# Expert queues of a routed feed-forward layer: full units of 512 slots, and half units of 256 at each queue's end

## The chip, the cores and the metric

One Trainium2 chip, one core. The metric is the device time of one execution in microseconds (us), the median over the runs shown; lower is better.

## The reference

50,000 rows of 256 numbers go through two layers. First a graph layer adds, to each row, the weighted normalised rows of its edges (25,000 edges, in fp16). Then a mixture of 8 experts is added. What the change touches is the second:

```python
logits = x @ gate_w + gate_b
probs = softmax(logits); idx = argmax(probs); prb = probs[idx]
pos = position of the token among those of its expert
kept = pos < C            # C = ceil(1.25 * 50000 / 8) = 7813
buf[e, pos] = x           # one queue per expert
hmid = relu(buf @ w1[e] + b1[e])      # 256 -> 1024
ybuf = hmid @ w2[e] + b2[e]           # 1024 -> 256
y = nan_to_num(ybuf[idx, pos] * prb * kept)
x = x + y
```

With the inputs of the reference, the eight queues hold 4993, 4159, 7813, 4367, 7813, 7813, 3828 and 2769 tokens (three are cut at C).

## The kernel before

The program has three stages. `edge_and_constants` does the graph layer. `route_tokens` computes logits for 1,024 rows a step and scatters each row, with its mean, its deviation, its token number and its logits, to a slot of its expert's queue in DRAM (`slots`). `run_experts` works the queues off. Only the third stage, and the last few VectorE (DVE) instructions of the second that count the units, are touched by the change.

A **unit** is 512 slots (`UNIT`, four blocks of 128, `SUB`). At the end of `route_tokens` DVE computes for each expert the number of units, ceil(queued / 512), their running sum (`first_unit`), the row at which each queue starts (`first_row`) and the row behind the last token (`first_blank`). For the queues above that is 10, 9, 16, 9, 16, 16, 8 and 6 units, 90 in all.

`run_experts` has one program for each engine, and each walks over experts and units alike: `experts` loads the expert's first and last unit number into registers (L881, L882), then `Fori(begin, end)` runs the body for each unit. The code of an expert stands six times in a row: for expert 0, twice inside a loop that runs two times, and for the last three. The engines meet through semaphores that count units, so nothing but the unit number tells an engine where it is. For unit u:

- **SyncE (SP)** keeps a ring of four units loaded (`load`, L906), and writes 512 blank slots behind the queue of the next expert (`blank_behind`, L900), so that a unit's unused slots have a token number out of range.
- **VectorE (DVE)** first normalises unit u+1 into `hn` (L1024, L1029). It then subtracts, for each of the eight column blocks f of the hidden layer, the rounded half of the hidden values from the full ones (`hlo`, L1047); then `xlo` of unit u+1 (L1036). Once TensorE has finished the second product it does the **tail**: bias (`y`, L1058), times probability (L1063), the three masks and `yo` for nan_to_num (L1067 to L1077), plus the residual (L1079), which releases the scatter.
- **TensorE (PE)** does the first product into `u_H` (L1114): 8 blocks of 6 matmuls with 512 columns, two PSUM buffers deep. Then it transposes unit u+1 (`u_T`, L1099, 8 matmuls), which waits for `hn` of u+1. Then the second product into `u_Y` (L1125): 8 blocks f, each 4 blocks of slots times 3 matmuls with 256 columns, which wait for `hlo`. Each fp32 product is three passes over rounded and rest parts.
- **ScalarE (ACT)** applies relu to each block of `u_H` (`hm`, L999), rounds it (`hhi`, L1003), and rounds the transposed unit u+1 (`xhi`, L983).
- **GpSimd (POOL)** scatters the unit's rows to the output with four indirect transfers (L967) and waits for their landing, which lets DVE overwrite the token numbers. Before the units of expert e it splits the weights of expert e+1: a cast of 128x4096 (`whi`, L943) and a subtraction (`wlo`, L945), then issues the loads of the weights of e+2.

Of the kernel before, what the change touches and what calls it, by code (L numbers as in the profile page):

```python
# [21 lines left out]
ALU = mybir.AluOpType  # L22
ACT = mybir.ActivationFunctionType
# [358 lines left out]
def route_tokens(nc, ctx, t):  # L382
# [66 lines left out]
    offset = sb("offset", [1, E], F32)  # L449
    first_unit, first_row, first_blank = t["first_unit"], t["first_row"], t["first_blank"]  # L450

# [23 lines left out]
    with nc.Block() as block:  # L475
# [149 lines left out]
        def _(v):  # L625
# [144 lines left out]
            v.tensor_reduce(count[:], over[:], AX.X, ALU.add).then_inc(step, n.inc())  # L770
            v.memset(begin[:], 0.0).then_inc(step, n.inc())
            v.wait_ge(step, n.now())
            for e in range(E):
                v.scalar_tensor_tensor(out=begin[:, e + 1:e + 2], in0=count[:, e:e + 1], scalar=1.0,
                                       in1=begin[:, e:e + 1], op0=ALU.max, op1=ALU.add).then_inc(step, n.inc())
                v.wait_ge(step, n.now())
            v.tensor_scalar(offset[:], expert[0:1, :], float(QUEUE), None, ALU.mult).then_inc(step, n.inc())
# [3 lines left out]
            v.wait_ge(step, n.now())  # L781
            v.tensor_copy(first_unit[:], begin[:])
            v.tensor_copy(first_row[:], offset[:])
# [3 lines left out]
def run_experts(nc, ctx, t):  # L787
# [9 lines left out]
    first_unit, first_row, first_blank = t["first_unit"], t["first_row"], t["first_blank"]  # L797
    E, D, F = w1.shape
# [6 lines left out]
    assert KF * D == WF and E >= 6 and E % 2 == 0  # L805
    HUGE = 1e4
# [14 lines left out]
    blank = sb("blank", [P, SUB, W], F32)  # L821
# [55 lines left out]
    def experts(eng, body):  # L877

        def one(e, buf):  # L880
            begin = eng.value_load(first_unit[0:1, bass.ds(e, 1)], min_val=0, max_val=(E - 1) * UMAX)  # L881
            end = eng.value_load(first_unit[0:1, bass.ds(e + 1, 1)], min_val=1, max_val=E * UMAX)  # L882
            body(e, buf, begin, end)
# [4 lines left out]
        for e in range(E - 3, E):  # L888
            one(e, e % 2)

    with nc.Block() as block:

        @block.sync
        def _(sp):
            sp.dma_start(b1r[:], b1.rearrange("e (k p) -> (e k) p", p=P)).then_inc(b1_loaded, 16)

            def blank_behind(e):

                row = sp.value_load(first_blank[0:1, bass.ds(e, 1)], min_val=0, max_val=E * QUEUE - UNIT)
                sp.dma_start(slots[bass.ds(row, UNIT), :].rearrange("(s p) w -> p s w", p=P), blank[:])\  # L900
                    .then_inc(blanked, 16)
# [7 lines left out]
            def expert(e, buf, begin, end):  # L909
# [6 lines left out]
                with sp.Fori(begin, end) as u:  # L916

                    sp.wait_ge(y_ready, u + (1 - RING + SEED["y_ready"]))
                    sp.nop(nofuse=True)
                    load(u, (u * UNIT + at).with_bounds(min_val=0, max_val=E * QUEUE - UNIT))  # L920
# [262 lines left out]
```

## Time and profile before

| | |
|---|---|
| median of 3 runs | 3663.58 us (3653.1 to 3665.04) |
| span of the profiled execution | 3533.8 us |
| PE busy | 2919.1 us (83%) |
| DVE busy | 2291.9 us (65%) |
| ACT busy | 1564.2 us (44%) |
| POOL busy | 1796.0 us (51%) |
| third stage, first to last instruction | about 1338 to 3534 us of the span |

No time of its own is listed for the profiled execution; the span runs from the first to the last instruction on the core, and the median of the runs lies 129.8 us above it. Busy time of a matmul counts from its start to a modelled end, and neighbours overlap; where a pace is wanted it is read from starts.

### The profile page before, as it was taken

The numbers are of one execution on the slowest core, as the hardware profiler recorded it, in microseconds if no ns is written. First come the engines' busy times: TensorE is split into PE (matmuls) and PEld (weight loads), VectorE is DVE, ScalarE is ACT, GpSimd is POOL, SyncE is SP. The second block draws the span as 40 slices with busy tenths as digits, with TensorE's granted clock in tenths as the row PEclk, the third lists the DMA queues.
The fourth block names the chain that finished last, engine by engine and source line by source line (L and its number), as shares of the span: only waits on it lengthen the run. The fifth ranks groups of instructions, "written<-read, shape, count | busy, mean of one in ns | idle before, by whom it ended". The sixth has DMA issues, their size and how long they took to land.

```text
span 3533.8 us, 60004 instructions
## 1 busy us (share of the span) xinstructions
PE 2919.1 (83%) x18982; PEld 2664.8 (75%) x18983; DVE 2291.9 (65%) x5804; ACT 1564.2 (44%) x2603; POOL 1796.0 (51%) x1195
## 2 busy tenths in 40 slices
PE   4544434078888876999999999999999999999998
PEld 3433434078888875988989988888988989998987
DVE  6655455077777764676676676676676676667666
ACT  2322222045555543554454555454555444454453
POOL 4788887647777773334343333434333433334332
PEclk8766666555555557999999999999999999999999
DMA  9544444399999963111111111111111121111110
GB/s 344 135 86 76 90 76 87 29 290 302 306 307 292 281 201 111 49 52 62 55 54 50 49 45 51 62 53 59 49 44 50 42 68 41 49 55 32 49 46 26
DMA packets 303467, 371.32 MB, mean 105 GB/s; under 512 B 35431, under 2 KB 263812, under 8 KB 300080
## 3 DMA queue, kind: packets, MB, share of 16 engines
q1 hardware_dynamic: 221504, 199.21, 19.2%
q0 software_dynamic: 78304, 145.23, 15.4%
q10 hardware_dynamic: 3600, 26.22, 1.8%
q8 instruction: 22, 0.36, 0.0%
q14 instruction: 37, 0.30, 0.0%
HBM read 184.33 MB, written 195.85 MB: 108 GB/s over the span
## 4 chain that ended last, share of the span: by engine, by line
PE 55%; DVE 3%; issue 2%; DVEq 1%; DMA 0%; SPq 0%; POOL 0%; ACT 0%; POOLq 0%; ACTq 0%
PE u_Y L1125 29%; PE u_H L1114 24%; PE u_T L1099 2%; DVE y L1058 1%; DVE yo L1077 1%; DVE yo L1074 0%; DVE y L1063 0%; DVE hn L1029 0%; DVE low L1068 0%; DVE hlo L1047 0%; DVE yo L1072 0%; DMA u_pay<-slots 0%; DMA slots<-blank 0%; DVEq L882 0%; DVEq L881 0%
## 5 line engine op out<-in xcount | busy, mean ns | idle before, releaser
L967 POOL DMA_INDIRECT out_x<-yo,u_token x360 | 712.3, 1979 | 1330.5 <-DVE yo L1079 1243.7
L1125 PE MATMUL u_Y<-whi,hhi 128*128 128x256 f32 x2880 | 816.0, 283 | 2.2 <-DVE hlo L1047 2.2
L999 ACT ACTIVATE hm<-u_H,b1e 128x512 f32<-128x512 f32 x720 | 496.3, 689 | 712.3 <-PE u_H L1114 684.0
L1125 PE MATMUL u_Y<-wlo,hhi 128*128 128x256 f32 x2880 | 807.2, 280 | 0.0
L1125 PE MATMUL u_Y<-whi,hlo 128*128 128x256 f32 x2880 | 806.2, 280 | 0.0
L1114 PE MATMUL u_H<-xhi,whi 128*128 128x512 f32 x1440 | 570.8, 396 | 3.1 <-DVE xlo L1036 2.5
L1114 PE MATMUL u_H<-xlo,whi 128*128 128x512 f32 x1440 | 570.3, 396 | 0.0
L1114 PE MATMUL u_H<-xhi,wlo 128*128 128x512 f32 x1440 | 570.0, 396 | 0.0
L1125 PEld LDWEIGHTS u_Y<-whi,hhi 128*128 128x128 f32 x2880 | 545.1, 189 | 2.4 <-DVE hlo L1047 2.4
L1125 PEld LDWEIGHTS u_Y<-wlo,hhi 128*128 128x128 f32 x2880 | 545.0, 189 | 0.0
L1125 PEld LDWEIGHTS u_Y<-whi,hlo 128*128 128x128 f32 x2880 | 544.3, 189 | 0.0
L534 POOL DMA_INDIRECT slots<-pay,slot_i x392 | 457.5, 1167 | 163.7 <-issue 122.5
L1058 DVE TENSOR_TENSOR y<-u_Y,b2e 128x256 f32<-128x256 f32 x360 | 127.7, 418 | 614.1 <-PE u_Y L1125 614.1
L1003 ACT ACTIVATE hhi<-hm 128x512 fp32r<-128x512 f32 x720 | 456.0, 633 | 22.9
L1047 DVE TENSOR_TENSOR hlo<-hm,hhi 128x512 fp32r<-128x512 f32 x720 | 452.7, 702 | 2.9 <-ACT hhi L1003 2.9
L212 POOL DMA_INDIRECT agg<-sums,target x200 | 328.5, 1642 | 79.2 <-issue 58.8
L599 PEld LDWEIGHTS ps_L<-gw,hT 128*128 128x128 f32 x1568 | 350.3, 332 | 0.1
L614 PE MATMUL ps_T<-ident,h 128*128 128x128 f32 x784 | 208.7, 431 | 167.3 <-ACT h L565 167.3
L599 PE MATMUL ps_L<-gw,hT 128*128 128x8 f32 x1568 | 342.4, 352 | 0.0
L1114 PEld LDWEIGHTS u_H<-xhi,whi 128*128 128x128 f32 x1440 | 271.0, 188 | 65.9 <-issue 4.1
L1114 PEld LDWEIGHTS u_H<-xhi,wlo 128*128 128x128 f32 x1440 | 270.9, 188 | 65.5
L1114 PEld LDWEIGHTS u_H<-xlo,whi 128*128 128x128 f32 x1440 | 271.0, 188 | 61.5
(127 smaller groups left out, 3757.4 us busy)
## 6 DMA issues: line engine op xcount, KB each, us to landing
xt<-in_x SPq DMA_DIRECT2D x49, 1024.0 KB
out_x<-pay SPq DMA_DIRECT2D x49, 1024.0 KB, 6.0
u_pay<-slots SPq DMA_DIRECT2D x91, 534.0 KB, 3.9
agg<-zeros ACTq DMA_DIRECT2D x25, 1024.0 KB, 10.9
at<-agg SPq DMA_DIRECT2D x49, 512.0 KB
raw<-in_L_ffn_w POOLq DMA_DIRECT2D x14, 1024.0 KB, 6.9
src_row<-in_src SPq DMA_DIRECT2D x25, 512.0 KB
slots<-pay,slot_i POOLq DMA_INDIRECT x392
```

The source lines that it names most:

```text
L212: pool.indirect_dma_start(out=agg[:, :], out_offset=bass.IndirectOffsetOnAxis(ap=target[:, r, c:c + 1], axis=0), in_=sums[:, r, c, :], in_ ...
L534: pool.indirect_dma_start(out=slots[:, :], out_offset=bass.IndirectOffsetOnAxis(ap=slot_i[:, r, g:g + 1], axis=0), in_=pay[:, r, g, :], in ...
L599: last = pe.matmul(logits[:, g, :], hT[:, g * KD + kd, :], gw[:, kd, :], start=(kd == 0), stop=(kd == KD - 1))
L614: last = pe.transpose(ps_T[:, n, :], h[:, q, g, kd * P:(kd + 1) * P], ident[:])
L967: pool.indirect_dma_start(out=out[:, :], out_offset=bass.IndirectOffsetOnAxis(ap=token[:, s:s + 1], axis=0), in_=yo[:, s, :], in_offset=No ...
L999: act.activation(hm[:, f, :], ps_H[:, f % 2, :], ACT.Relu, bias=b1e[:, f:f + 1])\
L1003: act.activation(hhi[:, f, :], hm[:, f, :], ACT.Copy).then_inc(hhi_ready, 1)
L1047: v.tensor_tensor(hlo[:, f, :], hm[:, f, :], hhi[:, f, :].bitcast(F32), ALU.subtract)\
L1058: last = v.tensor_tensor(y[:, s, :], ps_Y[:, s, 0:D], b2e[:], ALU.add)
L1099: last = pe.transpose(ps_T[:, k, s * P:(s + 1) * P], hn[:, s, k * P:(k + 1) * P], ident[:])
L1114: last = pe.matmul(ps_H[:, f % 2, :], w1_at(w, buf, k, f), a[:, k, :], start=(j == 0), stop=(j == len(passes) - 1))
L1125: last = pe.matmul(ps_Y[:, s, 0:D], a[:, f, cols], w2_at(w, buf, f), start=(f == 0 and j == 0), stop=(f == KF - 1 and j == 2))
```

## The change

Each queue is now worked off in full units of 512 slots followed by one or two half units of 256. DVE computes, beside the number c of 512-slot units, `wholes` = max(c - 1, 1) and `halves`, which is 2 where the last 512-slot unit would hold more than 256 tokens and else 1. Two new register tables go with it: `half_unit` (the number of the first half unit of each expert) and `half_row` (the row offset for half units). For the queues above the wholes are 9, 8, 15, 8, 15, 15, 7 and 5 (82), and the halves 2, 1, 1, 2, 1, 1, 1 and 1 (10).

Every engine's unit loop becomes two, with the body written out once for each size:

```diff
+    def units(eng, e, begin, end, unit):
+        half = eng.value_load(half_unit[0:1, bass.ds(e, 1)], min_val=1, max_val=E * (UMAX + 1))
+        with eng.Fori(begin, half) as u:
+            unit(u, SUB)
+        with eng.Fori(half, end) as u:
+            unit(u, SUB // 2)
```

In a half unit, first product, relu, rounding and `hlo` use 256 columns instead of 512; the second product, the tail and the scatter do two blocks of slots instead of four. What prepares unit u+1 stays at 512 slots in every unit: the load from `slots`, the normalisation, the eight transposes, `xhi` and `xlo`. The number of eight blocks f, and with it of ACT's and DVE's instructions on them, stays too. The blank stretch behind a queue grows from 512 to 768 slots.

```diff
-    blank = sb("blank", [P, SUB, W], F32)
+    blank = sb("blank", [P, BLANK // P, W], F32)
...
-                row = sp.value_load(first_blank[0:1, bass.ds(e, 1)], min_val=0, max_val=E * QUEUE - UNIT)
-                sp.dma_start(slots[bass.ds(row, UNIT), :].rearrange("(s p) w -> p s w", p=P), blank[:])\
+                row = sp.value_load(first_blank[0:1, bass.ds(e, 1)], min_val=0, max_val=E * QUEUE - BLANK)
+                sp.dma_start(slots[bass.ds(row, BLANK), :].rearrange("(s p) w -> p s w", p=P), blank[:])\
...
+                half = sp.value_load(half_unit[0:1, bass.ds(e, 1)], min_val=1, max_val=E * (UMAX + 1))
+                half_at = sp.value_load(half_row[0:1, bass.ds(e, 1)], min_val=0, max_val=E * QUEUE - UNIT)
+                with sp.Fori(begin, half) as u:
+                    unit(u, u * UNIT + at)
+                with sp.Fori(half, end) as u:
+                    unit(u, u * (UNIT // 2) + half_at)
...
-                    for s in range(SUB):
+                    for s in range(subs):
                         pool.indirect_dma_start(
                             out=out[:, :], out_offset=bass.IndirectOffsetOnAxis(ap=token[:, s:s + 1], axis=0),
                             in_=yo[:, s, :], in_offset=None, bounds_check=N - 1, oob_is_err=False,
-                        ).then_inc(y_sent, 16)
+                        ).then_inc(y_sent, 16 * SUB // subs)
...
-                        act.activation(hm[:, f, :], ps_H[:, f % 2, :], ACT.Relu, bias=b1e[:, f:f + 1])\
+                        act.activation(hm[:, f, cols], ps_H[:, f % 2, cols], ACT.Relu, bias=b1e[:, f:f + 1])\
...
-                        v.tensor_tensor(hlo[:, f, :], hm[:, f, :], hhi[:, f, :].bitcast(F32), ALU.subtract)\
+                        v.tensor_tensor(hlo[:, f, cols], hm[:, f, cols], hhi[:, f, cols].bitcast(F32), ALU.subtract)\
...
-                            last = pe.matmul(ps_H[:, f % 2, :], w1_at(w, buf, k, f), a[:, k, :],
+                            last = pe.matmul(ps_H[:, f % 2, cols], w1_at(w, buf, k, f), a[:, k, cols],
```

At the end of `route_tokens` DVE has ten more instructions on rows of 8 or 128 numbers of one partition.

Where the two loops meet, two places of the instruction streams. **GpSimd, from the scatter of one expert to the split of the next expert's weights** (`TENSOR_LOAD` reads a register from a table, `out_x<-yo` is the scatter). Before:

```order
L967 DMA out_x<-yo,u_token 50000x256 x4
L971 ISA
L963 REGISTER_ALU
L963 COMPARE_AND_BRANCH
L881 TENSOR_LOAD first_unit
L881 ISA x2
L882 ISA
L882 TENSOR_LOAD first_unit
L882 ISA x2
L941 REGISTER_ALU
L943 CAST whi<-raw 128x4096
L944 REGISTER_ALU
```

After, from the last scatter of the full units' loop on:

```order
L921 COMPARE_AND_BRANCH
L923 UNCONDITIONAL_BRANCH
L923 ISA
L1010 DMA out_x<-yo,u_token 50000x256 x2
L1014 ISA
L923 REGISTER_ALU
L923 COMPARE_AND_BRANCH
L907 TENSOR_LOAD first_unit
L907 ISA x2
L908 ISA
L908 TENSOR_LOAD first_unit
L908 ISA x2
```

The last scatter ahead of the cast has two transfers where it had four; the third register load (L920) stands behind the split, so it is not in its way.

**VectorE, the tail of a unit** (from the bias on `y` to the add that releases the scatter), before and then in the half units' loop:

```order
L1058 TENSOR_TENSOR y<-u_Y,b2e 128x256 x4
L1063 TENSOR_SCALAR y<-y,prob 128x256 x4
L1065 REGISTER_ALU
L1067 TENSOR_SCALAR finite<-y 128x1024
L1068 TENSOR_SCALAR low<-y 128x1024
L1071 ISA
L1071 COPY u_token<-u_pay 128x4
L1072 TENSOR_SCALAR yo<-y 128x1024
L1073 REGISTER_ALU
L1074 TENSOR_TENSOR yo<-yo,low 128x1024
```

```order
L1110 TENSOR_TENSOR y<-u_Y,b2e 128x256 x2
L1115 TENSOR_SCALAR y<-y,prob 128x256 x2
L1117 REGISTER_ALU
L1119 TENSOR_SCALAR finite<-y 128x512
L1120 TENSOR_SCALAR low<-y 128x512
L1123 ISA
L1123 COPY u_token<-u_pay 128x4
L1124 TENSOR_SCALAR yo<-y 128x512
L1125 REGISTER_ALU
L1126 TENSOR_TENSOR yo<-yo,low 128x512
```

All of the tail is half as wide, the copy of the token numbers apart; the order is the same.

## Rows read from the trace of the kernel before

**Rows 1.** The page, part 4: chain that ended last, by engine.
```profile
PE 55%; DVE 3%; issue 2%; DVEq 1%; DMA 0%; SPq 0%; POOL 0%; ACT 0%; POOLq 0%; ACTq 0%
```
**Rows 2.** Timeline of DVE, one unit: start us, us, engine line op out<-in xcount [idle before].
```profile
1572.78 1.42 DVE L1058 TENSOR_TENSOR y<-u_Y,b2e 128x256 f32<-128x256 f32 x4 [6.79 <-PE u_Y L1125]
1574.31 1.14 DVE L1063 TENSOR_SCALAR y<-y,prob 128x256 f32<-128x256 f32 x4
1575.48 0.69 DVE L1067 TENSOR_SCALAR finite<-y 128x1024 uint8<-128x1024 f32 x1
...
1578.82 1.37 DVE L1077 COPY_PREDICATED yo<-finite,y 128x1024 f32<-128x1024 uint8 x1
1580.31 1.23 DVE L1079 TENSOR_TENSOR yo<-yo,u_pay 128x1024 f32<-128x1024 f32 x1
1581.76 1.39 DVE L1029 TENSOR_SCALAR hn<-u_pay,scales 128x256 f32 x4
1583.05 4.91 DVE L1047 TENSOR_TENSOR hlo<-hm,hhi 128x512 fp32r<-128x512 f32 x8
...
1596.05 1.42 DVE L1058 TENSOR_TENSOR y<-u_Y,b2e 128x256 f32<-128x256 f32 x4 [6.78 <-PE u_Y L1125]
```
**Rows 3.** Timeline of PE's weight loads (PEld), the same unit.
```profile
1572.47 0.19 PEld L1114 LDWEIGHTS u_H<-xhi,whi 128*128 128x128 f32 x1
...
1583.55 1.02 PEld L1099 LDWEIGHTS u_T<-ident,hn 128*128 128x128 f32 x8
1584.54 0.19 PEld L1125 LDWEIGHTS u_Y<-whi,hhi 128*128 128x128 f32 x1
```
**Rows 4.** Groups of ACT in the third stage, window 1500 to 3534: busy, mean ns.
```profile
L999 ACT ACTIVATE hm<-u_H,b1e 128x512 f32<-128x512 f32 x672 | 463.2, 689 | 678.2 <-PE u_H L1114 651.7
L1003 ACT ACTIVATE hhi<-hm 128x512 fp32r<-128x512 f32 x672 | 425.6, 633 | 21.4
```
**Rows 5.** Timeline of POOL, from expert 1 to expert 2.
```profile
1824.93 5.16 POOL L967 DMA_INDIRECT out_x<-yo,u_token  x1 [0.30 <-issue]
1830.39 0.98 POOL L967 DMA_INDIRECT out_x<-yo,u_token  x1 [0.31 <-issue]
1834.07 3.61 POOL L943 CAST whi<-raw 128x4096 fp32r<-128x4096 f32 x1 [2.70 <-issue]
1837.77 9.13 POOL L945 TENSOR_TENSOR wlo<-raw,whi 128x4096 fp32r<-128x4096 f32 x1
```
**Rows 6.** Timeline of DVE at the same place.
```profile
1838.45 9.39 DVE L1063 TENSOR_SCALAR y<-y,prob 128x256 f32<-128x256 f32 x4
...
1870.59 1.42 DVE L1058 TENSOR_TENSOR y<-u_Y,b2e 128x256 f32<-128x256 f32 x4 [8.66 <-PE u_Y L1125]
```
**Rows 7.** Group of DVE's multiplications, window 1500 to 3534.
```profile
L1063 DVE TENSOR_SCALAR y<-y,prob 128x256 f32<-128x256 f32 x340 | 139.6, 474 | 9.1
```
**Rows 8.** Busy time by stretch: PE, PEld, DVE, ACT, POOL, granted clock, DMA.
```profile
1852.00:1856.00 4.00, 0.15 (x1) 0.15 (x2) 3.73 (x8) 0.00 (x0) 0.92 (x1) 0.50 1.01 340
```
**Rows 9.** Timeline of POOL and of DVE in the first unit of expert 0.
```profile
1367.88 9.33 POOL L945 TENSOR_TENSOR wlo<-raw,whi 128x4096 fp32r<-128x4096 f32 x1
1364.98 15.79 DVE L1047 TENSOR_TENSOR hlo<-hm,hhi 128x512 fp32r<-128x512 f32 x7 [1.27 <-ACT hhi L1003]
```
**Rows 10.** Timeline of POOL, one scatter from expert 0 to expert 1.
```profile
1609.91 1.50 POOL L967 DMA_INDIRECT out_x<-yo,u_token  x1 [0.30 <-issue]
```
**Rows 11.** Chain in order of time, start of the third stage.
```profile
1340.55 4.65 DMA slots<-blank
...
1346.39 0.28 SPq L915
```
**Rows 12.** Timeline of DVE and POOL, last unit.
```profile
3517.30 1.42 DVE L1058 TENSOR_TENSOR y<-u_Y,b2e 128x256 f32<-128x256 f32 x4 [6.78 <-PE u_Y L1125]
3526.83 0.98 POOL L967 DMA_INDIRECT out_x<-yo,u_token  x1 [14.19 <-DVE yo L1079]
...
3530.68 0.98 POOL L967 DMA_INDIRECT out_x<-yo,u_token  x1 [0.30 <-issue]
```

More of the change, by code:

```diff
@@ L781, in _ @@
             v.wait_ge(step, n.now())
+            v.scalar_tensor_tensor(out=half_at[:], in0=wholes[:], scalar=float(t["UNIT"] // 2), in1=offset[:],
+                                   op0=ALU.mult, op1=ALU.add).then_inc(step, n.inc())
+            v.wait_ge(step, n.now())
             v.tensor_copy(first_unit[:], begin[:])
+            v.tensor_copy(half_unit[:], wholes[:])
+            v.tensor_copy(half_row[:], half_at[:])
             v.tensor_copy(first_row[:], offset[:])
@@ L973, in expert @@
                     pool.sem_inc(y_clear, 1)
+                units(pool, e, begin, end, unit)
             experts(pool, expert)
@@ L988, in expert, with unit @@
                 act.nop(nofuse=True)
-                with act.Fori(begin, end) as u:
+                def unit(u, subs):
+                    cols = slice(0, subs * P)
                     act.wait_ge(hn_ready, u + 1)
@@ L1041, in expert, with unit @@
                 v.nop(nofuse=True)
-                with v.Fori(begin, end) as u:
+                def unit(u, subs):
+                    cols = slice(0, subs * P)
                     c = Count(u * PER)
@@ L1056, in expert @@
                     v.wait_ge(second_done, u + 1)
-                    for s in range(SUB):
+                    used = slice(0, subs)
+                    for s in range(subs):
                         last = v.tensor_tensor(y[:, s, :], ps_Y[:, s, 0:D], b2e[:], ALU.add)
@@ L1106, in expert, with unit @@
                 pe.nop(nofuse=True)
-                with pe.Fori(begin, end) as u:
+                def unit(u, subs):
+                    cols = slice(0, subs * P)
                     pe.wait_ge(x_ready, u + 1)
@@ L1121, in expert @@
                         pe.wait_ge(hid_ready, KF * u + (f + 1 + SEED["hid_ready"]))
-                        for s in range(SUB):
-                            cols = slice(s * P, (s + 1) * P)
+                        for s in range(subs):
+                            rows = slice(s * P, (s + 1) * P)
                             for j, (a, w) in enumerate(((hhi, whi), (hhi, wlo), (hlo, whi))):
-                                last = pe.matmul(ps_Y[:, s, 0:D], a[:, f, cols], w2_at(w, buf, f),
+                                last = pe.matmul(ps_Y[:, s, 0:D], a[:, f, rows], w2_at(w, buf, f),
                                                  start=(f == 0 and j == 0), stop=(f == KF - 1 and j == 2))
                     last.then_inc(second_done, 1)
+                units(pe, e, begin, end, unit)
             experts(pe, expert)
```

60 lines of the change are left out of this document (42 added, 18 removed).

## The prediction

> **What bounds the kernel now.** I read the page's chain first: 55% of the span is on PE, 3% on DVE [rows 1]. The change is in the third stage alone, so next comes the timeline of DVE over one unit [rows 2], where two units' first tail instructions lie 1596.05 - 1572.78 = 23.27 us apart. Almost all units have that period. PE's weight loads of the same unit fill it: 11.08 us of first product, 0.99 of transposes, then the second product until the next unit [rows 3]. But one DVE path is just as long. Counted from the start of a tail, the tail and the normalisation end at 1581.76 + 1.39 - 1572.78 = 10.4 us, and the transposes start at 10.8 [rows 2, 3]. So whatever makes DVE late in a full unit makes PE late by as much.
>
> That happens once for each expert. GpSimd splits the next expert's weights: cast and subtraction, until 1846.90 [rows 5]. DVE's multiplication of the tail starts at 1838.45 and takes 9.39 us instead of 1.14, until 1847.84 [rows 2, 6]. It waited for the subtraction, and the unit lasts from its tail at 1836.9 (1.5 before the multiplication, as in rows 2) to the one at 1870.59: 33.7 us, 10.4 too long, 8.25 of them the stall. PE, idle meanwhile, then has a granted clock of 0.50, the 1.2 GHz level [rows 8], so a little is lost on top. Over the stage, 340 such multiplications take 139.6 us [rows 7]; at 1.14 / 4 each they would take 96.9. So **42.7 us of stall** lie in the six splits after expert 0's, and with some 1.5 us of clock loss each (2.1 in the one above) the six units lose about 52.
>
> **The change, part by part.** T is the start of the tail of the unit before, on DVE.
>
> *A half unit behind a full one.* The tail in front is a full one, so the transposes can't start before T + 10.8, as now. The first product of 256 columns is done long before. PE would need 5.5 us; ACT's pair of relu and rounding takes 0.69 + 0.63 = 1.32 us at 512 columns [rows 4], 0.66 if all of it halves, 1.32 if nothing does. Even 8 x 1.32 = 10.6 fits in. So: 10.8 + 0.99 transposes + half of 11.2 for the second product (1584.54 to 1596.05, less 0.3 until DVE has started) + 0.3 = 17.7. PE is idle for some 3.5 us before its transposes. Between no loss and the 1.5 above I add 0.4: **18.1 us** instead of 23.27, bounds 17.7 and 19.2. It is not the 11.6 that half the work suggests.
>
> *A half unit behind a half one.* The tail halves. To the first mask it is 2.70 us, in which eight pieces of 128x256 become four: 1.4. From there to the copy (1575.48 to 1578.82) three masks and an add are halved: 3.34 - 3 x 0.27 - 0.53 = 2.0. The copy and the last add give 0.96 and 0.70 [rows 2]. A = T + 5.1 is when the scatter is released, instead of T + 8.8. Normalisation ends at T + 6.7, transposes can start at T + 7.1. ACT at 0.98 us a block, the middle of its bounds, lets PE finish at T + 7.0. Sum 7.1 + 0.99 + 5.6 + 0.3 = **14.0**.
>
> *Counts.* Six experts swap their last full unit for one half: 6 x (18.1 - 23.27) = **-31**. Experts 0 and 3 swap it for two: 2 x (18.1 + 14.0 - 23.27) = **+17.7**.
>
> *The split moves against DVE.* This is the largest term. Now the last scatter has four transfers, of which one waits 5.16 us for DVE's `hlo` series; the cast starts 2.7 us after the last one ends [rows 5]. In the change, the first transfer starts 0.8 us after A (the last unit: tail at 3517.30, transfer at 3526.83 [rows 12]), that is at T + 5.9; with 1.28 from transfer to transfer the second ends at T + 8.2. DVE is then still in its register loads, a third one now (0.55 us on SyncE [rows 11]), and the normalisation, so `hlo` starts only at about T + 8.9. The cast comes to the lock at T + 11.1. DVE is in the series of eight `hlo`, 4.9 us back to back [rows 2], until T + 13.8. I take it that the cast waits for its end, as the transfer of 5.16 us did. Then the cast runs to T + 17.5 and the subtraction to T + 26.7. The next tail starts at T + 23.8 and multiplies at T + 25.3: a stall of 1.4 us in place of 7.1 in the mean. Six times: 8.4 instead of 52, **-44**. Bounds: 0 if the cast slips in without harm (-52), 7 us each if it blocks `hlo` (below).
>
> *First unit of an expert.* It costs about 1 us over 23.27 now, as DVE has two register loads in the way. Its tail in front is now half as long, so DVE is early; but PE's own third load (0.55) comes between two products. -0.5 each, seven times: **-3.5**.
>
> *Start of the stage.* The blank transfer of 534 KB lands in 4.65 us and the first load waits for it [rows 11]; 801 KB take between 4.65 and 7.0, I take +1.3. Wiping the blank tile: +0.4. Two register loads of SyncE at 0.55: +1.1. Together **+2.8**. DVE's ten new instructions at the end of the second stage lie under GpSimd's last scatters, which keep the stage open some 19 us longer: 0.
>
> *End.* The tail is 3.7 shorter and two transfers of 1.28 fall away: **-6.2** [rows 12].
>
> Sum: -31 + 17.7 - 44 - 3.5 + 2.8 - 6.2 = **-64.2**. Against the profiled execution that is 3533.8 - 64.2 = 3469.6 of span; against the median, 129.8 above the span, 3599.4, say **3600 us**. That the part outside the span stays is an assumption; the program is longer by half on PE.
>
> **Rivals.**
> 1. *The cast breaks into the `hlo` series.* In the first unit of expert 0, seven `hlo` take 15.79 us under cast and subtraction [rows 9]: that is 11.5 more than their 0.61 each, longer than the subtraction's 9.33, so the cast blocks them as well. And one scatter transfer got through a series in 1.50 us [rows 10]. If so, `hlo` of the last three blocks waits until the subtraction ends at T + 24, where PE wants the sixth at T + 19: about 5.6 us idle, plus clock, 7 each in place of 1.4. +33.6: 3633 us. For it: DVE's series is eight instructions, with an edge between each two. Against it: most scatter transfers wait the whole series out, as in rows 5. The Trainium skill ("SBUF — State Buffer", section "Who interferes with whom") says that whoever of the two issues first holds the shared pair for a whole instruction; read strictly, the waiting cast would get in after the `hlo` that is running, which is this rival. The 5.16 us transfer speaks against reading it so.
> 2. *A half unit costs as much as a full one*, since its fixed parts (full preparation of the next unit, ACT's per-instruction part) bound it. Then 8 x 5.2 + 2 x 9.3 = 60 us come back: 3660, no change. ACT's pair would have to take 2.5 us at half the width, against 1.32 now.
> 3. *Slower: the granted clock falls in the half unit and stays down.* In it PE works in bursts (ACT sets the pace) and is then idle until T + 10.8. If the lower level lasted through the half unit's transposes and second product, these 6.6 us would double, and the next first product's 11.1 too: 17.7 us for each of eight experts, 142 in all, 3741 us. It decides the sign from 64 / 8 = 8 us of doubled work for each expert on. Against it: after a longer idle time the level of 0.50 shows [rows 8], and the 10 us lost there are mostly the 8.25 of stall. The Trainium skill ("TensorE: Matmul & The Clock Gate", section "A second HAM failure mode: psum-queue depth-cycling") reports that short pauses between matmul groups on cycling PSUM buffers can make the clock swing. The trace before has no group of this kind; by that section the half units' first product would bring it.
> 4. *The change doesn't do what it says:* no. 82 + 10 units follow from the queues, and the streams show both loops.
>
> **Numbers.** Forecast 0.60 (its own range 3585 to 3617, from the bounds of the half units, 17.7 to 19.2, the split without harm, the start and the runs' spread of some 6 us). Rival 1 0.28. Rival 2 0.04. Rival 3 0.03. Something unlisted, such as code of twelve loops fetched late or a longer part outside the span, 0.05. The range reaches down to 3580 and up to rival 1 with the dearer half unit, 3645. A change of under 0.3% (11 us) can't be told from none here. Faster: forecast, rival 1 and most of the unlisted, 0.92. Same: rival 2 and a little, 0.05. Slower: rival 3, 0.03.
>
> **What the profile of the changed kernel would show.** Tails 23.27 us apart in full units, about 18.1 into the first half unit, 14.0 into the second. Half-width relu and rounding together near 0.98 us. POOL's cast starts some 11 to 14 us after a half tail. DVE's multiplications with full width near 0.3 us in the mean instead of 0.41, none above 2.5 us. If instead `hlo` instructions of over 9 us appear once for each expert, rival 1 holds. A granted clock below 1.00 in more than a short stretch for each half unit speaks for rival 3. Wrong altogether would be tails after half units over 23 us apart, or an unchanged sum of rows 7.

## The result, and the profile after

| | before | changed |
|---|---|---|
| median | 3660.99 us (4 runs) | 3562.68 us (4 runs, 3555.91 to 3572.21) |
| ratio, 95% interval | | 0.9741 (0.9716 to 0.9766) |
| span of the profiled execution | 3533.8 us | 3567.3 us |
| first instruction of the third stage's DVE, in the span | 1338.44 | 1466.00 |
| third stage, from there to the end | 2195.4 us | 2101.3 us |

The change makes the kernel 98 us faster (2.6%). I had forecast 3600 us, 64 us faster, with a range of 3580 to 3645; the measured time lies 17 us below it.

The two profiled executions can't be compared by their spans. The second stage, which the change hardly touches, ends 128 us later in the profile of the changed kernel. Where both kernels were profiled side by side, their third stages start alike (1332.4 and 1332.6 us in the first group of runs below). In two other groups both start later: at 1422 to 1430 us with the kernel before as a basis, at 1417 to 1432 with the changed one. So this difference goes with the group of runs and not with the change; what makes it is not known (the chip's number alone does not: of the two groups on the chip numbered 12, one starts at 1331 to 1335, the other at 1424 to 1432). It also shows that my 129.8 us "around the span" were not around it: each later execution lists a time 1 to 2 us above its span (here 3569.06 to 3567.3). The third stages can be compared (with the tiles of the kernel before at the old distance it took 2194.5 to 2196.0 us in three groups of runs), and they differ by 94 us.

One full unit on DVE, then the first and the second half unit of expert 0, in the timeline of the changed kernel (start us, us, engine line op out<-in xcount, idle time before):

```profile
1653.15 1.42 DVE L1110 TENSOR_TENSOR y<-u_Y,b2e 128x256 f32<-128x256 f32 x4 [6.26 <-PE u_Y L1181]
...
1698.67 1.42 DVE L1110 TENSOR_TENSOR y<-u_Y,b2e 128x256 f32<-128x256 f32 x4 [6.26 <-PE u_Y L1181]
...
1707.58 1.38 DVE L1078 TENSOR_SCALAR hn<-u_pay,scales 128x256 f32 x4
1708.87 2.77 DVE L1098 TENSOR_TENSOR hlo<-hm,hhi 128x256 fp32r<-128x256 f32 x8
...
1717.21 0.76 DVE L1110 TENSOR_TENSOR y<-u_Y,b2e 128x256 f32<-128x256 f32 x2 [4.26 <-PE u_Y L1181]
...
1721.62 0.69 DVE L1131 TENSOR_TENSOR yo<-yo,u_pay 128x512 f32<-128x512 f32 x1
...
1722.54 1.39 DVE L1078 TENSOR_SCALAR hn<-u_pay,scales 128x256 f32 x4
...
1730.77 0.76 DVE L1110 TENSOR_TENSOR y<-u_Y,b2e 128x256 f32<-128x256 f32 x2 [2.85 <-PE u_Y L1181]
```

Against [rows 2]: the first half unit lasts 1717.21 - 1698.67 = 18.5 us, the second 13.6. The normalisation behind a full tail still ends at +10.3, behind a half tail at +6.7. The half tail releases the scatter at 1721.62 + 0.69, +5.1. The first half unit is within the forecast's bounds, the ends of the normalisation are as forecast. But the next tail behind the one at 1653.15 stands at 1675.91: **full units are 22.76 us apart, not 23.27**. PE's weight loads show where the half microsecond went:

```profile
1652.84 0.19 PEld L1170 LDWEIGHTS u_H<-xhi,whi 128*128 128x128 f32 x1
1663.71 0.14 PEld L1153 LDWEIGHTS u_T<-ident,hn 128*128 128x128 f32 x1
...
1664.70 0.19 PEld L1181 LDWEIGHTS u_Y<-whi,hhi 128*128 128x128 f32 x1
...
1675.60 0.19 PEld L1170 LDWEIGHTS u_H<-xhi,whi 128*128 128x128 f32 x1
```

The first product takes 10.87 us for 11.08 [rows 3], the second 10.90 for 11.2, the transposes the same 0.99. No instruction of a full unit differs between the kernels. I had not considered that PE's pace could differ all the same.

The split of the next expert's weights, at the same place as [rows 5, 6], from expert 0's last half unit (tail at 1730.77) on, first GpSimd and then DVE:

```profile
1738.01 0.99 POOL L1010 DMA_INDIRECT out_x<-yo,u_token  x1 [0.30 <-issue]
1742.26 5.62 POOL L985 CAST whi<-raw 128x4096 fp32r<-128x4096 f32 x1 [3.26 <-issue]
1747.96 9.38 POOL L987 TENSOR_TENSOR wlo<-raw,whi 128x4096 fp32r<-128x4096 f32 x1
...
1740.10 8.32 DVE L1098 TENSOR_TENSOR hlo<-hm,hhi 128x512 fp32r<-128x512 f32 x8
...
1754.69 1.42 DVE L1110 TENSOR_TENSOR y<-u_Y,b2e 128x256 f32<-128x256 f32 x4 [4.96 <-PE u_Y L1181]
1756.22 2.07 DVE L1115 TENSOR_SCALAR y<-y,prob 128x256 f32<-128x256 f32 x4
```

The cast comes at +11.5 (forecast +11.1) and lasts 5.62 instead of 3.61: it waits 2.0 us for `hlo`, where the forecast had 2.7. But it gets in ahead of the eighth one: the series takes 8.32 us instead of 4.90. The multiplication is held for under 1 us. Over the stage the group of [rows 7] now reads

```profile
L1115 DVE TENSOR_SCALAR y<-y,prob 128x256 f32<-128x256 f32 x348 | 105.1, 365 | 9.9
```

which is 6 us above 348 times 0.285, where it was 42.7.

In the half units behind full ones PE waits 4.3 us for `hn` and the granted clock goes down at about the end of the wait, to the 1.2 GHz level for part of this stretch (the stretch's mean is 0.71):

```profile
1709.01 0.97 PEld L1153 LDWEIGHTS u_T<-ident,hn 128*128 128x128 f32 x8 [4.31 <-DVE hn L1078]
1708.00:1712.00 4.00, 2.98 (x17) 2.99 (x18) 4.00 (x13) 1.03 (x1) 3.49 (x2) 0.71 0.60 170
```

### The profile page after: what moved, and what is told of

Same layout as the page of the kernel before. It is cut to its first block, busy times and chain, and to the rows that moved or that the text cites. A ratio compares the mean times of both kernels' runs of the same rounds, so it can differ in the third digit from the quotient of the medians.

```text
span 3567.3 us, 60077 instructions
## 1 busy us (share of the span) xinstructions
PE 2846.6 (80%) x18806; PEld 2603.9 (73%) x18807; DVE 2245.0 (63%) x5836; ACT 1539.7 (43%) x2638; POOL 1724.4 (48%) x1183
## 4 chain that ended last, share of the span: by engine, by line
PE 53%; DVE 4%; issue 1%; DVEq 0%; DMA 0%; SPq 0%; ACT 0%; POOL 0%; POOLq 0%; ACTq 0%
PE u_Y L1181 27%; PE u_H L1170 23%; PE u_T L1153 3%; DVE y L1110 1%; DVE yo L1129 1%; DVE yo L1126 1%; DVE y L1115 0%; DVE hn L1078 0%; DVE low L1120 0%; DVE hlo L1098 0%; DVE yo L1124 0%; DMA slots<-blank 0%; DMA u_pay<-slots 0%; DVE scales L1073 0%; DVEq L1078 0%
## 5 line engine op out<-in xcount | busy, mean ns | idle before, releaser
L1010 POOL DMA_INDIRECT out_x<-yo,u_token x348 | 668.5, 1921 | 1261.4 <-DVE yo L1131 1179.5
L1181 PE MATMUL u_Y<-whi,hhi 128*128 128x256 f32 x2784 | 784.2, 282 | 1.5 <-DVE hlo L1098 1.5
L1181 PE MATMUL u_Y<-wlo,hhi 128*128 128x256 f32 x2784 | 775.4, 279 | 0.0
L1046 ACT ACTIVATE hm<-u_H,b1e 128x512 f32<-128x512 f32 (+1 forms) x736 | 487.9, 663 | 639.8 <-PE u_H L1170 627.0
L539 POOL DMA_INDIRECT slots<-pay,slot_i x392 | 415.3, 1059 | 325.5 <-DVE slot_i L748 210.3
L1170 PE MATMUL u_H<-xhi,whi 128*128 128x512 f32 (+1 forms) x1472 | 563.6, 383 | 8.0 <-issue 5.5
L1170 PE MATMUL u_H<-xhi,wlo 128*128 128x512 f32 (+1 forms) x1472 | 562.2, 382 | 0.0
L1170 PE MATMUL u_H<-xlo,whi 128*128 128x512 f32 (+1 forms) x1472 | 560.2, 381 | 0.0
L1050 ACT ACTIVATE hhi<-hm 128x512 fp32r<-128x512 f32 (+1 forms) x736 | 448.7, 610 | 23.3
L1098 DVE TENSOR_TENSOR hlo<-hm,hhi 128x512 fp32r<-128x512 f32 (+1 forms) x736 | 454.0, 692 | 2.9 <-ACT hhi L1050 2.9
L604 PE MATMUL ps_L<-gw,hT 128*128 128x8 f32 x1568 | 344.0, 353 | 39.8 <-ACT hT L566 24.5
L1170 PEld LDWEIGHTS u_H<-xhi,wlo 128*128 128x128 f32 x1472 | 277.4, 188 | 50.4
```

The lines of the kernel that those rows point to most:

```text
L539: pool.indirect_dma_start(out=slots[:, :], out_offset=bass.IndirectOffsetOnAxis(ap=slot_i[:, r, g:g + 1], axis=0), in_=pay[:, r, g, :], in ...
L604: last = pe.matmul(logits[:, g, :], hT[:, g * KD + kd, :], gw[:, kd, :], start=(kd == 0), stop=(kd == KD - 1))
L1010: pool.indirect_dma_start(out=out[:, :], out_offset=bass.IndirectOffsetOnAxis(ap=token[:, s:s + 1], axis=0), in_=yo[:, s, :], in_offset=No ...
L1046: act.activation(hm[:, f, cols], ps_H[:, f % 2, cols], ACT.Relu, bias=b1e[:, f:f + 1])\
L1050: act.activation(hhi[:, f, cols], hm[:, f, cols], ACT.Copy).then_inc(hhi_ready, 1)
L1098: v.tensor_tensor(hlo[:, f, cols], hm[:, f, cols], hhi[:, f, cols].bitcast(F32), ALU.subtract)\
```

## The experiments

Kernels of one group ran on one chip, beside the kernel before. "Stage" is the third stage from its first DVE instruction to the end of the span; "units" the time from the first tail to the last.

### The pace of PE: four kernels on one chip

**The kernel before, again** (no edit).

> The kernel before, unchanged, profiled on the chip of the other three runs. Theory P (placement): PE's pace belongs to the program, so full units are again 23.27 us apart and PE's weight loads of the second product 0.117 us apart. Rival C (chip): the pace belongs to the chip or the execution, so here full units come at 22.76, as in the profile of the changed kernel. Both: the second stage, which the two profiles show at 1338 and about 1470 us of the span's start to its end, is as long as in the other runs here, and the span is some 3660.

Ratio 0.9998 (0.9989 to 1.0008), 3529.78 us; stage 2196.0 us, full units 23.27. The expected span of 3660 was missed: in this group the second stage is short for all kernels.

**The kernel before, tiles moved:**

```diff
-        for name, n in (("first_unit", E + 1), ("first_row", E), ("first_blank", E)):
+        for name, n in (("first_unit", E + 1), ("first_row", E), ("first_blank", E),
+                        ("half_unit", E), ("half_row", E)):
...
     blank = sb("blank", [P, SUB, W], F32)
+    pad = sb("pad", [P, 534], F32)
```

> The kernel before, with two unused tables of 32 bytes and an unused tile of 2,136 bytes a partition, so that every tile of the third stage lies at the SBUF address that it has in the changed kernel; no instruction differs. Theory P: full units 22.76 us apart instead of 23.27, 90 x 0.51 = 46 us faster than before, ratio about 0.987. Rival C: ratio 1.000.

Ratio 0.9878 (0.9862 to 0.9895), 3488.06 us, stage 2158.9. PE's weight loads and DVE's tails of this kernel:

```profile
1493.76 0.19 PEld L1115 LDWEIGHTS u_H<-xhi,whi 128*128 128x128 f32 x1
...
1504.63 0.14 PEld L1100 LDWEIGHTS u_T<-ident,hn 128*128 128x128 f32 x1
1505.62 0.19 PEld L1126 LDWEIGHTS u_Y<-whi,hhi 128*128 128x128 f32 x1
...
1516.52 0.19 PEld L1115 LDWEIGHTS u_H<-xhi,whi 128*128 128x128 f32 x1
```
```profile
1516.83 1.42 DVE L1059 TENSOR_TENSOR y<-u_Y,b2e 128x256 f32<-128x256 f32 x4 [6.28 <-PE u_Y L1126]
```

10.87, 0.99, 10.90, and the tail before stood 22.76 us earlier, with every instruction of the kernel before. Theory P holds and rival C is out: the two unused tables and the unused tile alone are worth 42 us.

**The changed kernel, again** (no edit).

> The changed kernel, unchanged. Both theories: ratio 0.974, full units at 22.76.

Ratio 0.9736 (0.972 to 0.9753), 3437.55 us, stage 2104.9.

**The changed kernel, tiles moved back:**

```diff
-        for name, n in (("first_unit", E + 1), ("first_row", E), ("first_blank", E),
-                        ("half_unit", E), ("half_row", E)):
+        for name, n in (("first_unit", E + 1), ("first_row", E), ("first_blank", E)):
...
         t["wlo"] = outer.enter_context(nc.sbuf_tensor("wlo", [P, 2, 2 * WF], F32R))
+        for name, n in (("half_unit", E), ("half_row", E)):
+            t[name] = outer.enter_context(nc.sbuf_tensor(name, [1, n], I32))
...
-    blank = sb("blank", [P, BLANK // P, W], F32)
+    pad = sb("pad", [P, 1056], F32)
...
     yo = sb("yo", [P, SUB, D], F32)
+    blank = sb("blank", [P, BLANK // P, W], F32)
```

> The changed kernel with its tiles of the third stage back at the addresses of the kernel before (the two tables behind the weights, the blank tile behind all others, a pad in its place). Theory P: full units back at 23.27, 82 x 0.51 = 42 us and some 3 for the half units slower than the changed kernel, ratio to before about 0.986, so the loops alone are worth some 52 us. Rival C: ratio 0.974 as without the move.

Ratio 0.9834 (0.9818 to 0.9851), 3471.51 us, stage 2139.9: full units at 23.27 again. This is the change by its loops alone: **59 us, 1.7%**; the prediction had 64, the expectation above 52. The placement is worth 34 us here (3471.51 to 3437.55) and not the 45 expected, and 42 in the kernel before. Only units that PE bounds get shorter with it: most full units by 0.51 us, but the half units behind full ones took 19.16 us in the mean with the old addresses and 19.06 with the new ones, and the second units of experts 1 to 6 took 23.6 and 23.8. Its first half unit, then expert 1's first and second unit:

```profile
1572.33 1.42 DVE L1111 TENSOR_TENSOR y<-u_Y,b2e 128x256 f32<-128x256 f32 x4 [6.82 <-PE u_Y L1182]
...
1590.99 0.76 DVE L1111 TENSOR_TENSOR y<-u_Y,b2e 128x256 f32<-128x256 f32 x2 [3.94 <-PE u_Y L1182]
...
1604.46 0.75 DVE L1111 TENSOR_TENSOR y<-u_Y,b2e 128x256 f32<-128x256 f32 x2 [2.80 <-PE u_Y L1182]
...
1628.92 1.42 DVE L1111 TENSOR_TENSOR y<-u_Y,b2e 128x256 f32<-128x256 f32 x4 [5.49 <-PE u_Y L1182]
1630.44 1.53 DVE L1116 TENSOR_SCALAR y<-y,prob 128x256 f32<-128x256 f32 x4
1652.37 1.42 DVE L1111 TENSOR_TENSOR y<-u_Y,b2e 128x256 f32<-128x256 f32 x4 [6.26 <-PE u_Y L1182]
```
```profile
1582.68 1.57 PEld L1154 LDWEIGHTS u_T<-ident,hn 128*128 128x128 f32 x8 [4.27 <-DVE hn L1079]
```

These units last 18.7, 13.5, 24.5 and 23.4 us. The eight transposes take 1.57 us instead of 0.99 behind an idle time of 4.27.

### What it is about the addresses

Weights (`whi`, `wlo`) and activations (`xhi`, `xlo`, `hhi`, `hlo`) are the two operands of every matmul. All pairs of one matmul lie at the same distance modulo 512 bytes, 224 in the kernel before, since every slice and every tile among them is a multiple of 512 long. Seven variants of the kernel before, five of them run once, for the profile: six with an edit of the form

```diff
     blank = sb("blank", [P, SUB, W], F32)
+    pad = sb("pad", [P, 8], F32)
```

with 8, 16, 536, 256, 24 and 40 numbers of 4 bytes, and one with the two tables alone.

> The kernel before with an unused tile of 32 bytes a partition ahead of the activation tiles of the third stage: xhi, xlo, hhi, hlo start 32 bytes further (135200 instead of 135168 for xhi, and so on), the weights stay. Theory A: what slows the matmuls is that these tiles start at multiples of 4096 bytes; any shift ends it: full units 22.76 us, ratio 0.988. Theory B: it is the address modulo 64 (0 before, 32 in the changed kernel): here 32 too, ratio 0.988, and no gain at a shift of 64. Theory W: it is the weights' shift of 64 bytes: ratio 1.000.

> The same with 64 bytes instead of 32. Theory A: 22.76 us, ratio 0.988. Theory B: still 23.27, ratio 1.000. Theory W: 1.000.

> The kernel before with the two unused tables alone: weights and activation tiles both 64 bytes further. Theory D (only the distance between weights and activation tiles matters): as before, 23.27 us, weight loads 0.233 and 0.117 us apart. Theory E (the absolute addresses matter): another period.

> The kernel before with activation tiles 2,144 bytes further and the weights in place: the distance of the changed kernel at other absolute addresses. Theory D: 22.76 us. Theory E: another period.

> The kernel before with activation tiles 1,024 bytes further. No theory gives a number: if the period is again 23.27, whole kilobytes change nothing; if it is near 22.76, the large shift is what counts.

> The kernel before with activation tiles 96 bytes further. Theory M (what matters is the distance between weights and activations modulo 512 bytes or a divisor of it, as the pairs of one matmul all lie a multiple of 512 apart): it is 224 before, 224 at +1,024 and with both moved, 320 in the changed kernel and at +2,144, 256 at +32, 288 at +64; +96 gives 320, so 22.76 us with weight loads 0.230 and 0.1135 apart. Otherwise (the large shift counts): another period.

> The kernel before with activation tiles 160 bytes further, 384 modulo 512 and 0 modulo 128. If the pattern repeats every 128 bytes: the paces of +32 (0.227 and 0.120 us, 23.30 us in all). If it repeats every 256 or 512 only, other paces.

| activations further by | distance mod 512 | first product, us | second product, us | full unit, us |
|---|---|---|---|---|
| 0 (before) | 224 | 11.08 | 11.20 | 23.27 |
| 0, weights and activations both 64 | 224 | | | 23.27 |
| 1,024 | 224 | | | 23.27 |
| 32 | 256 | 10.80 | 11.51 | 23.30 |
| 64 | 288 | 11.08 | 11.36 | 23.43 |
| 96 | 320 | 10.87 | 10.90 | 22.76 |
| 2,144 | 320 | | | 22.76 |
| 2,144, both 64 more (as in the changed kernel) | 320 | 10.87 | 10.90 | 22.76 |
| 160 | 384 | 11.03 | 11.38 | 23.40 |

Theories A, B and W fall with the rows of 32 and 64, E with the tables alone, and D (the distance) and M (its value modulo 512) hold in all nine rows. A pad of 96 bytes gives the whole effect. At 384 the first product differs from that at 256, so the pattern doesn't repeat every 128 bytes, and 288 differs from 224 in the second product, so not every 64. Whether it repeats every 256 wasn't run. Nor was a shift of exactly 512: the two pairs of rows that agree lie 1,024 and 2,048 bytes apart. The two variants that were timed several times say the same in time: 1.0011 (0.9997 to 1.0025) at 32 and 1.0038 (1.0023 to 1.0053) at 64. Why a distance of 320 is good was not settled, nor whether a better one exists; five distances were tried.

The pad moves all tiles behind it against all tiles ahead of it, so the runs don't prove that weights and activations are the pair that counts. That PE waits for another engine is unlikely, for the difference is spread evenly over each product. In the kernel before, the starts of the 48 matmuls of the first product lie 232 and 235 ns apart in turn, from its beginning to its end (medians over 90 units); with the tiles moved they lie 226, 229 and 232 ns apart. In the second product the steps are 116, 117, 120 and 113 before, and 113 from the sixth step on when moved. What DVE and ACT do changes several times over such a product.

The Trainium skill ("TensorE: Matmul & The Clock Gate", section "Step-by-step: what each phase is for") says that PE reads its streaming operand and its weights through two independent ports, so that loading the next tile takes nothing from the running matmul. If the two operands are the pair that counts here, 10.80 to 11.08 us for the same 48 matmuls don't agree with that; no run shows the mechanism.

### The place of the split

**The cast held back**, in the changed kernel:

```diff
+                    pool.wait_ge(prob_ready, begin + 1 + SEED["prob_ready"])
+                    pool.nop(nofuse=True)
                     split_weights(e + 1, 1 - buf)
```

> The changed kernel, but GpSimd holds the cast of the next expert's weights until DVE has done the reciprocal of the expert's first unit, some 16.5 us behind the last half unit's tail start instead of 11.5. Theory S (the gain of the change is mostly that the split leaves DVE's multiplication free): the subtraction then ends at +29.4, the multiplication that starts at +25.3 stalls for 4 us, and the second unit of an expert lasts 27 to 28.5 us instead of 23.3 to 24.5: 6 x 4 = 24 us slower than the changed kernel, ratio to before about 0.980. Rival: the split's place is worth nothing and the stalls went for another reason: 0.974.

GpSimd and DVE from expert 0 to expert 1 (tail at 1697.7):

```profile
1713.74 3.62 POOL L985 CAST whi<-raw 128x4096 fp32r<-128x4096 f32 x1 [7.80 <-DVE prob L1107]
1717.44 9.07 POOL L987 TENSOR_TENSOR wlo<-raw,whi 128x4096 fp32r<-128x4096 f32 x1
...
1721.64 1.42 DVE L1112 TENSOR_TENSOR y<-u_Y,b2e 128x256 f32<-128x256 f32 x4 [8.16 <-PE u_Y L1183]
1723.17 4.28 DVE L1117 TENSOR_SCALAR y<-y,prob 128x256 f32<-128x256 f32 x4
```

The subtraction ends at 1726.51, the multiplication waits for it (4.28 for 1.14), and the second units of the six experts last 26.1 to 29.1 us (29.05, 26.25, 26.34, 26.12, 26.08, 27.14; 23.3 to 24.5 in the changed kernel). Stage 2118.7 for 2101.3 and 2104.9: 14 to 17 us more. The ratio, 0.9805 (0.9772 to 0.9838), is at the forecast 0.980. So a cast that starts 4.5 us later (+16.0 for +11.5) costs some 3 us for each expert: theory S holds, and its rival at 0.974 lies outside the interval. The effect was sized too high (24 us): the multiplication is held for 3.1 us here and not 4.0, and in the changed kernel it is already held for 0.9.

### A half unit bound by the tail in front of it

**The normalisation a unit further ahead**, in the changed kernel:

```diff
-                    normalise(u + 1)
...
                     v.reciprocal(prob[:], total[:]).then_inc(prob_ready, 1)
+                    normalise(u + 2)
```

(with a normalisation of unit 1 ahead of the loops, and one more load at the end of SyncE's program).

> The changed kernel with one more unit of lead for the normalisation: DVE normalises unit u+2 before it waits for the second product of unit u, in its idle time, instead of u+1 behind the tail. Theory H (a half unit behind a full one is bound by tail and normalisation, after which PE's transposes start at +10.3): the transposes start at once, at +6, and the half unit's second product then waits for hlo at +9: 14.6 to 15 us instead of 18.3 to 19.6, 8 x 4 = 32 us, and 1 us less in first and second units of an expert: some 40 us faster than the changed kernel, ratio about 0.962. Rival (the half unit is bound by ACT or by the lower clock): 0.974.

The tails of expert 0's first half unit, of the second, and behind it; then GpSimd and DVE in expert 1's first unit (tail at 1689.72):

```profile
1660.61 1.42 DVE L1115 TENSOR_TENSOR y<-u_Y,b2e 128x256 f32<-128x256 f32 x4 [6.28 <-PE u_Y L1188]
...
1677.10 0.76 DVE L1115 TENSOR_TENSOR y<-u_Y,b2e 128x256 f32<-128x256 f32 x2 [2.19 <-PE u_Y L1188]
...
1689.72 0.76 DVE L1115 TENSOR_TENSOR y<-u_Y,b2e 128x256 f32<-128x256 f32 x2 [1.49 <-PE u_Y L1188]
```
```profile
1666.60 0.90 PEld L1160 LDWEIGHTS u_T<-ident,hn 128*128 128x128 f32 x8
...
1701.17 3.61 POOL L990 CAST whi<-raw 128x4096 fp32r<-128x4096 f32 x1 [3.23 <-issue]
1704.87 9.31 POOL L992 TENSOR_TENSOR wlo<-raw,whi 128x4096 fp32r<-128x4096 f32 x1
...
1701.96 12.77 DVE L1102 TENSOR_TENSOR hlo<-hm,hhi 128x512 fp32r<-128x512 f32 x2 [0.68 <-ACT hhi L1055]
```

Half units behind full ones take 15.4 to 16.6 us, and the transposes start at +6.0 (1666.60 - 1660.61): theory H is right on the path, but the half units are 0.4 to 2 us longer than the expected 14.6 to 15. The longer ones, 16.5 us, are those in which the granted clock shows 0.50 for 3.4 us. And the first units of the six experts that have a split in them grow to 27.6 to 28.5 us, so that the ratio of 0.962 is missed. `hlo` runs here as its inputs come, with gaps, the cast slips into one at its usual 3.61 us, and two `hlo` take 12.77 us behind cast and subtraction. That is the prediction's rival 1, on a kernel where it costs 4 us an expert. Stage 2092.3, ratio 0.9711 (0.9675 to 0.9747).

**With the held cast as well** (this edit and the one before it together):

> The changed kernel with both edits of the two runs before: the normalisation one unit further ahead, and the cast of the next weights held until the reciprocal of the expert's first unit. If the first units of 27.6 to 28.5 us in the early normalisation's run come from hlo blocked by the subtraction, they go back to about 23.5 here, and the stall of the multiplication (3.5 us) no longer reaches PE, since PE's transposes no longer wait behind it: second units 22.8 to 23.5. Six experts gain 4 us each over the early normalisation alone: 24 to 27 us, ratio about 0.964. Rival (the long first units have another cause, such as loop entry): 0.971 or worse.

Ratio 0.9723 (0.9691 to 0.9756), stage 2098.4: a miss. No `hlo` is blocked any more, but the early normalisation stands where the subtraction now runs, and takes 13.62 us instead of 1.38; the first tail of each of these six experts comes 28.5 to 29.5 us behind the tail before it.

**The normalisation between bias add and multiplication**, with and without a hold of the cast until the first unit's last `hlo`:

```diff
                     last.then_inc(y_read, 1)
+                    normalise(u + 2)
```

The hold:

```diff
+                    pool.wait_ge(hid_ready, begin * KF + (KF + SEED["hid_ready"]))
+                    pool.nop(nofuse=True)
                     split_weights(e + 1, 1 - buf)
```

> The changed kernel with the normalisation of unit u+2 between the bias add and the multiplication of unit u's tail, and the cast held until the expert's first unit has its eighth hlo. PE's transposes then never wait (they can start at +6 in a half unit), while hlo starts at about +10.3 as in the changed kernel: a half unit behind a full one 16.8 us plus up to 1 of clock loss instead of 18.3 to 19.6. The split lies at +14 to +27, blocks no hlo, and holds the multiplication 1.5 us, which PE no longer sees: first and second units of an expert 23.5 and 22.8. Some 20 us faster than the changed kernel, ratio 0.968, which would also beat the early normalisation (0.971). If the long first units there had another cause than the blocked hlo, they stay at 28 here and the ratio is 0.976.

> The same without the hold. hlo is a series again of eight back to back, from +9 to +14, because the tail's second half and the normalisation lie ahead of it, so the cast should wait for its seventh, as in the changed kernel, and block only the eighth: ratio 0.968 as with the hold. If the cast gets in earlier (as with the early normalisation, where hlo had gaps), first units of 27 to 28 us and 0.975.

Held: 0.9721 (0.9705 to 0.9738), stage 2091.4. Without: **0.9704 (0.9688 to 0.972)**, 3426.72 us, stage 2089.8. Both intervals lie above the expected 0.968. GpSimd and DVE from expert 0 to 1 in the latter (tail at 1599.19):

```profile
1612.00 3.88 POOL L990 CAST whi<-raw 128x4096 fp32r<-128x4096 f32 x1 [3.19 <-issue]
1615.96 9.38 POOL L992 TENSOR_TENSOR wlo<-raw,whi 128x4096 fp32r<-128x4096 f32 x1
...
1608.10 4.30 DVE L1102 TENSOR_TENSOR hlo<-hm,hhi 128x512 fp32r<-128x512 f32 x7 [0.96 <-ACT hhi L1055]
1612.80 3.62 DVE L1102 TENSOR_TENSOR hlo<-hm,hhi 128x512 fp32r<-128x512 f32 x1 [0.40 <-ACT hhi L1055]
...
1623.19 1.42 DVE L1114 TENSOR_TENSOR y<-u_Y,b2e 128x256 f32<-128x256 f32 x4 [5.45 <-PE u_Y L1188]
```

`hlo` is back to back up to the seventh, the cast blocks the eighth alone, first units take 23.6 to 24.4 us (with the hold 23.5 to 24.3). Half units behind full ones take 16.2 to 19.1 us, on which the clock decides: 16.2 where the granted clock stays at 1.00, the rest where it shows 0.50 for some 3.4 or 6.8 us. Seven of the eight show such a fall, and the mean is 17.8 us, the upper end of what was expected; first and second units of an expert, 23.9 and 23.3 us in the mean, are each some 0.5 us longer than expected. The long first units of the early normalisation thus came from the blocked `hlo`. This version has the lowest ratio of all that were run; its interval overlaps those of the other three with an early normalisation, so that it can't be told from them. Its stage is 15 us shorter than that of the changed kernel; of the times, the intervals of the two (0.9688 to 0.972 and 0.972 to 0.9753) just meet, in two groups of runs.

## Why the prediction was right or wrong

The direction was right. The size was too small and the range missed, because one effect was not in it at all. **The step that failed: every step of the sum takes the full unit to be 23.27 us long after the change too, a term put at nothing without a reason.** What the runs showed in its place is 22.76 us, since the longer `blank` tile moves the activation tiles against the weights; this is worth 42 us in the kernel before and 34 in the changed one.

The other terms are compared below by the tails of the changed kernel moved back to the old addresses, beside the kernel before in the same group.

- **Six single half units:** -31 forecast. The eight half units behind full ones took 18.46 to 19.67 us, 19.16 in the mean, for 18.1; so -24.7. The path was as I described it, with two sizes off. The transposes start at +10.34 and not at +10.8: in a full unit the 10.8 is the end of the first product (11.08 us from -0.31), and `hn` is ready at +10.4. And the term for the clock was too small: with transposes at +10.34 the sum is 17.2 us, so 1.2 to 2.4 us were lost where 0.4 stood, with a granted clock of 0.50 for 3.4 or 6.8 us about the end of 4.3 us idle.
- **Two experts with two halves:** +17.7 forecast, +18.8 measured; the second half units take 13.5 for 14.0. PE waits 0.67 us for `hn` in them and starts the transposes at +6.74; the forecast had them 0.4 us behind the normalisation, the same misreading of the full unit. ACT's pair takes 0.46 + 0.42 = 0.88 us at 256 columns (0.98 forecast), and ACT is not what PE waits for there.
- **The split:** -44 forecast. Second units of experts 1 to 6 were 53.1 us over 23.27 in all before, 2.1 now: -51. The cast waited for most of the `hlo` series, the subtraction ended at +26.2 to +27.1 (forecast +26.7), and the first tail came at +23.9 to +24.7, a little later than I had it, so there was almost nothing left to hold (1.53 us for a multiplication of 1.14 in the lines above). It is the largest term, and the held cast shows that the place of the split makes it.
- **First units of an expert:** -3.5 forecast, 0 measured (24.2 us in the mean in both). The bound changes engines. Expert 1's first unit starts with the tail at 1589.62 in the kernel before and at 1604.46 in the changed one moved back; PE's first weight load of the first product and of the transposes in each:

```profile
1589.75 0.19 PEld L1114 LDWEIGHTS u_H<-xhi,whi 128*128 128x128 f32 x1 [0.37 <-issue]
1601.78 0.31 PEld L1099 LDWEIGHTS u_T<-ident,hn 128*128 128x128 f32 x3 [1.01 <-DVE hn L1029]
```
```profile
1605.33 0.19 PEld L1171 LDWEIGHTS u_H<-xhi,whi 128*128 128x128 f32 x1 [1.10 <-issue]
1616.41 0.14 PEld L1154 LDWEIGHTS u_T<-ident,hn 128*128 128x128 f32 x1
```

  Before, PE waits 1.01 us for `hn`, until +12.2. In the changed kernel `hn` is ready at +9.4, but PE starts its first product at +0.87 instead of +0.13, and the transposes follow it without a wait at +11.95. What it does in the 1.10 us before is not shown; its stream there has the third register load. The eighth `hlo`, done at +17.7, plays no part: PE comes to its eighth block at +22.7.
- **Start:** +2.8 forecast, +4.8 measured (first tail 47.8 and 52.6 us into the stage). The blank transfer lands in 5.79 us in the changed kernel's profile, for 4.65, and wiping the tile takes 1.39 for 0.95, both as forecast. The rest can't be told from the spread: the same way took 50.6 and 51.8 us in the changed kernel's two profiles, and 47.5 to 50.4 in those of the kernel before and its variants.
- **End:** -6.2 forecast, -3.4 measured. The tail is 3.7 shorter; but 3.28 us of idle time lie between the last two transfers, where I had 0.30. What fills them is not shown.
- **Sum of the loops:** -64.2 forecast, 2196.0 - 2139.9 = -56.1 of stage and -59 of time.
- **Not in the sum:** the placement. The diff showed the longer `blank` tile; I priced its transfer and its wiping, and not what it moves.

That the loops alone came within 5 us of the forecast (8 in the stage) is in part luck: the split gave 7 us more than its term, and the half units, the first units, the start and the end together some 16 us less than theirs.

Rival 1 came true in part: in four or five of six experts the cast gets in before the eighth `hlo`. That one then ends at +17.7 instead of about +14.2, and PE needs it only at +22.7, so it costs nothing. With gaps in the series it costs 4 us. The strict reading of the section "Who interferes with whom" of the Trainium skill ("SBUF — State Buffer"), that the waiting cast would get in after the running `hlo`, is not what was seen in the changed kernel: the cast of the lines above waited for 2 us, over three of them. Rivals 2 and 3 didn't come true: the clock fell in each half unit behind a full one, but for 3.4 to 6.8 us and not beyond; the second half units, whose first product has pauses for ACT, show no fall at all, so the swing that the Trainium skill describes ("TensorE: Matmul & The Clock Gate", section "A second HAM failure mode: psum-queue depth-cycling") is not seen here.

To take the 129.8 us for time outside the span was an error of reading. It had no effect on the size of the forecast, as they were carried over unchanged.

## What to carry to other kernels

Before a change in tile sizes is judged, look at whether the operands of the hot matmuls move against each other in SBUF; a variant of the kernel before with the same addresses separates the two effects in one run. A pad of 96 bytes alone took the full unit of the kernel before from 23.27 to 22.76 us. A half-size unit saves only what isn't bound by the full-size unit in front of it. And where two engines exclude each other, a saved microsecond of queue in front of the long instruction can be worth more than the work saved.

## What the runs showed of the hardware that was not expected

- The same matmuls took 10.80 to 11.08 us (48 with 512 columns) and 10.90 to 11.51 us (96 with 256 columns) as the tiles behind the pad, their activations among them, were shifted against the weights by 0 to 160 bytes; shifts of 1,024 and of 2,144 bytes gave what 0 and 96 gave. The eight transposes took 0.99 to 1.00 us in all.
- The order isn't the same for both: of the five distances, 256 is the best distance for the first product and the worst for the second.
- A GpSimd cast that waits for DVE's series of two-operand subtractions got in before its eighth instruction in 13 of 18 cases, after waits of 0.6 to 2.2 us; in the other five it waited 2.3 to 2.8 us, over the whole series. Where the series had gaps it got in at once (six of six).
- Of the 360 scatter transfers in the kernel before, 85 took 5.0 to 5.2 us instead of 0.98. All of them overlap such a series.
- Two indirect transfers at the end of the program lay 4.26 us apart, where four had lain 1.28 apart each.
